# One loop in place of three for two graph layers, with the LSTM's first unit inside it

## The chip, the cores and the metric

The kernel runs on one NeuronCore of a Trainium2 chip. The metric is the device time of one execution in microseconds (us). The engines meant below are TensorE (PE in the rows; its weight loads are PEld), VectorE (DVE), ScalarE (ACT) and GpSimd (POOL). Each works through its own list of instructions in order and waits for the others at semaphores.

## The reference

`x` is 32 x 256 x 128 in fp32 (32 batches, 256 nodes, 128 features) and `adj` is 256 x 256. Two layers are added to x one after the other, each behind a layer norm and a relu. U holds the eigenvectors of the normalised Laplacian of `adj`; the second layer is two graph products and then four LSTMs over windows of nodes:

```python
h = jnp.maximum(_layernorm(x, axis=-1), 0.0)
agg = jnp.einsum('mn,bnd->bmd', U.T, h)
x = x + jnp.einsum('nm,bmd->bnd', U, jax.nn.relu(agg @ W1 + b1) @ W2 + b2)
h = jnp.maximum(_layernorm(x, axis=-1), 0.0)
h = jax.nn.relu(jnp.einsum('ts,bsh->bth', adj, h @ Wg0 + bg0))
h = jax.nn.relu(jnp.einsum('ts,bsh->bth', adj, h @ Wg1 + bg1))
for p in range(1, MAX_SKIP + 1):
    ...
    last = _lstm_last(Wih[p - 1], Whh[p - 1], bih[p - 1], bhh[p - 1], wins)
    ...
    h = h.at[:, idx, :].set(last.reshape(Bv, nw, Hd))
x = x + h
```

`wins` are the windows of p neighbouring nodes (`MAX_SKIP` is 4), and `idx` the last node of each.

## The kernel before

The eigenvectors take the kernel's first 1,128 us: tridiagonalisation, root finding, back-transformation. The change leaves that part alone. What follows are three stages, all in fp32, and all held in SBUF.

**Units of work.** The 32 batches go in 16 pairs (`PAIRS`) and 8 groups of four (`GROUPS`). Every matmul that the program asks for shows as two records in the trace. Three kinds of work stand on TensorE:

- an aggregation: for one pair, H of the pair times a 256 x 256 matrix, eight records of 256 columns (line 791, whatever the matrix: U in the first layer, adj transposed in the second);
- a weight product: for one pair, the evacuated aggregation times a 128 x 128 weight, eight records of 128 columns (line 807 in the first layer, 833 in the second's first half), or two of 512 columns (line 846 in its second half);
- an eigenvector product: for one group, UT times O, eight records of 512 columns in two halves, one PSUM bank each (line 818).

**First layer**, lines 798 to 819. In step c TensorE issues aggregation c, weight product c-1, and at odd c from 3 the eigenvector product of group (c-3)/2. ScalarE evacuates each aggregation with bias and relu (line 560). VectorE adds the bias of each weight product (line 1324, semaphore `l0_os`), adds the eigenvector product into X (1332), and takes the second layer norm's statistics of a group (1338 to 1343). ScalarE takes the root (564), and VectorE normalises the group one odd step later (`norm2`, lines 1311 to 1318); ScalarE then applies the relu (569). The eigenvector product of a group waits for `l0_os` of its two pairs, the second of which is the weight product issued just ahead of it:

```python
if c >= 3 and c % 2:
    gr = (c - 3) // 2
    pe.wait_ge(S["l0_os"], 2 * gr + 2)
```

**Second layer**, lines 821 to 846: a loop of 17 steps for each half, each with aggregation c and weight product c-1. On ScalarE, one step of the first half is the evacuation of aggregation c (line 572) and then the relu of pair c (574), which is there only when weight product c is done and VectorE has added its bias (1348):

```python
act.wait_ge(S["l1_agg"], c + 1)
a(aggs[:, c % 2], bank[c % 2][:], ACT.Copy).then_inc(S["l1_aggs"], 1)
act.wait_ge(S["l1_ys"], c + 1)
a(H[:, :, 2 * c:2 * c + 2], H[:, :, 2 * c:2 * c + 2], ACT.Relu).then_inc(S["l1_y"], 1)
```

The second half does the same with lines 577, 1352 and 580.

**LSTM**, lines 855 to 879. Units of work (one pair, one window length p, one step t) go in a fixed order, four pairs in turn. Unit u on TensorE is three gate products (four at t > 0) of 256 columns or fewer; ScalarE applies the gate functions (592) and, one unit later, the tanh of the cell (599); VectorE multiplies (1388 to 1394) and writes the hidden state (1371, 1373). The first four units wait for the relu of all 16 pairs; a later one waits for the unit four before it.

Of the kernel before, what the change touches and what calls it, by code (L numbers as in the profile page):

```python
# [33 lines left out]
def gnn_kernel(nc, x, adj, W1, b1, W2, b2, Wg0, bg0, Wg1, bg1, Wih, Whh, bih, bhh, out):  # L34
# [34 lines left out]
    with ExitStack() as ctx:  # L69
# [353 lines left out]
        def _(act):  # L423
# [131 lines left out]
            for c in range(PAIRS + 5):  # L555
# [9 lines left out]
                if c >= 6 and c % 2 == 0:  # L565
                    gr = (c - 6) // 2
# [8 lines left out]
            for c in range(PAIRS):  # L575
                act.wait_ge(S["l1_agg2"], c + 1)
                a(aggs[:, c % 2], bank[4 + c % 2][:], ACT.Copy).then_inc(S["l1_agg2s"], 1)
                act.wait_ge(S["l1_zs"], c + 1)
                v = HT[:, 2 * c:2 * c + 2]
                a(v, v, ACT.Relu).then_inc(S["l1_z"], 1)  # L580
# [22 lines left out]
        def _(pe):  # L603
# [182 lines left out]

            def aggregate(dst, c, M):
# [8 lines left out]
            for c in range(PAIRS + 2):  # L796
# [4 lines left out]
                if 1 <= c <= PAIRS:  # L801
                    e = c - 1
                    pe.wait_ge(S["l0_hids"], e + 1)
                    if e >= 2:
                        pe.wait_ge(S["l0_os"], e - 1)
                    for j in range(4):
                        last = mm(bank[4 + e % 2][:, j * P:(j + 1) * P], hid[:, e % 2, j * P:(j + 1) * P], W2s[:], start=True, stop=True)
                    last.then_inc(S["l0_o"], 1)
                if c >= 3 and c % 2:
                    gr = (c - 3) // 2  # L810
# [9 lines left out]

            for c in range(PAIRS + 1):
                if c < PAIRS:
                    pe.wait_ge(S["ln2_relu"], c + 1)
                    if c >= 2:
                        pe.wait_ge(S["l1_aggs"], c - 1)
                    aggregate(c % 2, c, adjT).then_inc(S["l1_agg"], 1)
                if c >= 1:
                    e = c - 1
                    pe.wait_ge(S["l1_aggs"], e + 1)
# [5 lines left out]
            for c in range(PAIRS + 1):  # L835
                if c < PAIRS:
                    pe.wait_ge(S["l1_y"], c + 1)
                    if c >= 2:
                        pe.wait_ge(S["l1_agg2s"], c - 1)
                    aggregate(4 + c % 2, c, adjT).then_inc(S["l1_agg2"], 1)  # L840
                if c >= 1:
                    e = c - 1
# [12 lines left out]
            pe.wait_ge(S["wlt_cp"], 8)  # L855
            for u, (gr, (p, t, part), q) in enumerate(UNITS):
                c = SLOTS * gr + q
                n = 256 if p == 1 else 2 * (N // p)
                if u < SLOTS:
                    pe.wait_ge(S["l1_z"], PAIRS)  # L860
                else:
                    pe.wait_ge(S["gate_act"], u + 1 - SLOTS)
                    if p > 1:
                        pe.wait_ge(S["h_rdy"], u + 1 - SLOTS)
                if (p, t) == (3, 0):
                    pe.wait_ge(S["third_rdy"], gr + 1)
# [555 lines left out]
```

## Time and profile before

| what | value |
|---|---|
| median of 3 runs | 1660.71 us (1658.88 to 1660.86) |
| the profiled execution's own time | 1660.92 us |
| its span in the trace, first to last instruction | 1658.9 us |
| first aggregation of the first layer (line 791) | 1128.2 us from the span's start |
| first gate function of the LSTM (line 592) | 1325.14 us |
| mean granted TensorE clock | 0.94 of full speed |

The stages that the change touches take the 197 us between the two marks of the fourth and fifth row. Times in rows are in us from the start of the span. In a timeline row the first number is the start, the second the length (to the end of the last of the xN instructions, for matmuls with the time in which the result leaves the array), and the bracket says how long the engine sat idle before it and who released it.

### The profile page before, as it was taken

The page shows a single profiled execution, that of the slowest core. Times are in us where ns is not written, and L with a number is a line of the kernel's source. Part 1 is how long each engine was busy: PE and PEld are TensorE (multiplying, and loading weights), DVE is VectorE, ACT ScalarE, POOL GpSimd, SP SyncE. Part 2 cuts the span into 40 slices and gives each one's busy share as a digit, 9 for nine tenths or more (in the row PEclk, how much of TensorE's full clock was granted, in tenths as well). Part 3 has the DMA queues.
Part 4 walks back from the last instruction along what each step waited for, and adds up shares of the span by engine and source line. Part 5 has one row for each costly group of instructions (what it writes and reads, how often), then busy time and mean ns, then how long its engine had stood idle before and what let it go on. Part 6 is the DMA issues. An engine that isn't in the chain of part 4 may idle for free.

```text
span 1658.9 us, 25312 instructions
## 1 busy us (share of the span) xinstructions
PE 1289.4 (78%) x5985; PEld 1068.8 (64%) x5985; DVE 1259.3 (76%) x6154; ACT 609.9 (37%) x2116; POOL 397.7 (24%) x2138
## 2 busy tenths in 40 slices
PE   6999999999976667777264444519878899999997
PEld 5777888888865555555143333507656588889897
DVE  7898988888888888888999999993732255555555
ACT  1222222222233444222121212402223386868676
POOL 5333333333345555555100000120000011000100
PEclk9999999999999999999887775769989999999999
DMA  7000000000000000000000000000000000000001
GB/s 166 1 1 1 1 1 1 2 1 1 2 1 1 1 1 1 1 1 1 0 1 0 1 0 1 1 0 1 1 1 1 0 1 1 1 1 26 1 27 52
DMA packets 23402, 12.64 MB, mean 8 GB/s; under 512 B 5075, under 2 KB 22230, under 8 KB 23254
## 3 DMA queue, kind: packets, MB, share of 16 engines
q1 hardware_dynamic: 23254, 11.03, 2.7%
q8 instruction: 48, 0.79, 0.2%
q14 instruction: 100, 0.82, 0.2%
HBM read 6.83 MB, written 4.19 MB: 7 GB/s over the span
## 4 chain that ended last, share of the span: by engine, by line
DVE 47%; PE 33%; issue 9%; POOL 6%; ACT 4%; DVEq 1%; POOLq 0%
PE bank L873 10%; PE bank L875 6%; DVE A L1001 4%; DVE RC L1089 4%; PE bank L647 3%; DVE O L1097 3%; PE bank L650 3%; DVE O L983 3%; DVE pa L1085 3%; DVE O L1093 2%; DVE junk L953 2%; DVE zc L995 2%; DVE wk L987 2%; PE bank L791 2%; PE bank L818 2%
## 5 line engine op out<-in xcount | busy, mean ns | idle before, releaser
L592 ACT ACTIVATE H<-bank,gate_b 128x128 f32<-128x128 f32 (+2 forms) x624 | 213.4, 438 | 81.9 <-PE bank L875 79.3
L650 PEld LDWEIGHTS bank<-O 128*128 128x128 f32 x764 | 201.3, 344 | 0.0
L873 PE MATMUL bank<-O,WlT 128*128 128x128 f32 (+1 forms) x896 | 192.0, 328 | 7.8 <-DVE O L1366 5.6
L659 PE MATMUL bank<-O,y 128*128 128x2 f32 x510 | 142.4, 349 | 65.5 <-DVE y L953 59.7
L647 PE MATMUL bank<-ident,O 128*128 128x128 f32 x382 | 148.2, 457 | 47.6 <-DVE O L983 35.6
L467 ACT ACTIVATE ncp<-pc,RC 128x2 f32<-128x2 f32 (+1 forms) x254 | 74.9, 295 | 292.4 <-DVE RC L974 292.4
L659 PEld LDWEIGHTS bank<-O,y 128*128 128x128 f32 x510 | 128.4, 312 | 77.5 <-issue 72.4
L875 PE MATMUL bank<-H,WlT 128*128 128x128 f32 (+2 forms) x768 | 169.1, 301 | 0.0
L873 PEld LDWEIGHTS bank<-O,WlT 128*128 128x128 f32 x896 | 148.1, 192 | 24.6 <-issue 7.3
L650 PE MATMUL bank<-O 128*128 128x1 f32 x764 | 162.7, 305 | 0.0
L667 PE MATMUL bank<-ident,pc 128*128 128x128 f32 x381 | 147.7, 456 | 5.4 <-DVE pc L972 2.2
L647 PEld LDWEIGHTS bank<-ident,O 128*128 128x128 f32 x382 | 60.1, 198 | 135.2 <-DVE O L983 135.2
L463 ACT ACTIVATE root<-bank 128x1 f32<-128x1 f32 x255 | 43.7, 171 | 260.1 <-PE bank L650 260.1
L735 PE MATMUL bank<-chg,fold 128*128 128x512 bf16 x64 | 28.6, 571 | 139.4 <-DVE chg L1047 139.4
L309 POOL TENSOR_TENSOR ym<-y,below 128x2 f32<-128x2 f32 (+1 forms) x254 | 49.1, 193 | 349.7 <-DVE y L961 251.8
L875 PEld LDWEIGHTS bank<-H,WlT 128*128 128x128 f32 x768 | 124.7, 189 | 3.3
L991 DVE SCALAR_TENSOR_TENSOR A<-bank,cx,A 128x254 f32<-128x254 f32 (+63 forms) x380 | 121.2, 319 | 0.4 <-issue 0.4
L418 POOL COPY Wl<-O 128x344 f32<-128x344 f32 (+1 forms) x24 | 17.2, 763 | 421.3 <-DVE O L1371 421.3
L1001 DVE SCALAR_TENSOR_TENSOR A<-bank,zc,A 128x254 f32<-128x254 f32 (+63 forms) x380 | 111.7, 321 | 4.5
L1391 DVE TENSOR_TENSOR H<-H 128x128 f32<-128x128 f32 (+2 forms) x96 | 31.6, 329 | 106.6 <-ACT H L592 106.6
L508 ACT ACTIVATE sgn<-O 128x1024 bf16<-128x1024 f32 (+1 forms) x24 | 32.2, 1342 | 205.4 <-DVE O L1097 205.4
L735 PEld LDWEIGHTS bank<-chg,fold 128*128 128x128 bf16 x64 | 5.5, 116 | 150.9 <-DVE chg L1047 121.0
(381 smaller groups left out, 3059.2 us busy)
## 6 DMA issues: line engine op xcount, KB each, us to landing
X<-in_x SPq DMA_DIRECT2D x2, 2048.0 KB, 13.9
out<-X SPq DMA_DIRECT2D x32, 128.0 KB, 1.9
adj_sb<-in_adj SPq DMA_DIRECT2D x1, 256.0 KB, 3.0
W1s<-in_L_gnn_W SPq DMA_DIRECT2D x1, 64.0 KB, 10.2
W2s<-in_L_gnn_W SPq DMA_DIRECT2D x1, 64.0 KB, 3.2
Wg0s<-in_L_gnn_Wg SPq DMA_DIRECT2D x1, 64.0 KB, 3.0
Wg1s<-in_L_gnn_Wg SPq DMA_DIRECT2D x1, 64.0 KB, 3.6
Wl<-in_L_gnn_Wih SPq DMA_DIRECT2D x1, 0.5 KB, 6.6
```

Of the source, the lines that this page charges most:

```text
L467: a(ncp[:, bs], pc[:, bs], ACT.Identity, scale=RC[:, k, 1:2]).then_inc(S["ncp_ready"], 1)
L592: ins = a(gates[:, q, i, 0:n], gate_at(p, q, i), fn, bias=gate_b[:, p - 1, i:i + 1])
L647: ins = nc.tensor.transpose(xb[:, b * P:(b + 1) * P], R[:, b, k, 0:1].to_broadcast([P, P]), idf)
L650: ins = mm(bank[0][:, 0:1], R[:, b, k, 0:1].to_broadcast([P, P]), R[:, b, k, 0:1], start=(b == bl[0]), stop=(b == 1))
L659: ins = mm(sb_[:, 0:2], y[:, 1:2].to_broadcast([P, P]), R[:, 1, k, :], start=True, stop=(k >= P - 1))
L667: ins = nc.tensor.transpose(bank[5][:, b * P:(b + 1) * P], pc[:, b:b + 1].to_broadcast([P, P]), idf)
L873: last = mm(gate_at(p, q, i), WlT[:, 0, p - 1, i, :], window(c, p, t, part), start=True, stop=(t == 0))
L875: last = mm(gate_at(p, q, i), WlT[:, 1, p - 1, i, :], hst[:, q, 0:n], start=False, stop=True)
L983: stt(out=R[:, bs, k + 1, 0], in0=cx[:, bs], scalar=gqn[:], in1=tm[:, bs], op0=ALU.mult, op1=ALU.subtract, reverse1=True).then_inc(S["x_re ...
L991: stt(out=A[:, b, c0 + 1:e], in0=bank[5][:, c0 + 1:e], scalar=cx[:, b:b + 1], in1=A[:, b, c0 + 1:e], op0=ALU.mult, op1=ALU.add).then_inc(S ...
L1001: stt(out=A[:, b, c0 + 1:e], in0=xb[:, c0 + 1:e], scalar=zc[:, b:b + 1], in1=A[:, b, c0 + 1:e], op0=ALU.mult, op1=ALU.add).then_inc(S["upd ...
L1089: mark(stt(out=pb2[:, :, 0:w], in0=lam2, scalar=dbh[:, BLK + j:BLK + j + 1], in1=pair(j, w), op0=ALU.subtract, op1=ALU.mult))
```

## The change

One loop over 3 x 16 + 1 steps takes the place of the three loops on TensorE, ScalarE and VectorE (the last two with slightly different bounds). The first layer is steps 0 to 16 and more, the second layer's halves start at steps 16 and 32. Within it:

- the eigenvector product of group g moves from odd step 2g+3, behind the weight product, to even step 2g+4, behind the aggregation and ahead of the weight product;
- on VectorE the two additions of the eigenvector product stand ahead of the bias addition (line 1324) and the statistics in the even step; ScalarE's roots move to odd steps, VectorE's `norm2` to odd steps from 5, behind the bias addition;
- in the second layer, ScalarE's relu of a pair stands two steps behind the evacuation of the same pair, not right behind it;
- the next half's aggregations start while the last weight products, and at the first seam the last eigenvector products and layer norms, are still to come;
- gate products of unit 0 are issued ahead of the last weight product; units 1 to 3 wait for the relu of their own pair and for the last reader of their banks.

No instruction that computes is added or removed. The diff, cut where the same edit is repeated:

```diff
@@ ScalarE @@
-            for c in range(PAIRS + 5):
+            for c in range(3 * PAIRS + 2):
                 if c < PAIRS:
                     ...
-                if c >= 4 and c % 2 == 0 and (c - 4) // 2 < GROUPS:
-                    gr = (c - 4) // 2
+                if PAIRS <= c < 2 * PAIRS:
+                    i = c - PAIRS
+                    act.wait_ge(S["l1_agg"], i + 1)
+                    if i >= 2:
+                        act.wait_ge(S["l1_y_ps"], i - 1)
+                    a(aggs[:, i % 2], bank[i % 2][:], ACT.Copy).then_inc(S["l1_aggs"], 1)
+                if 2 * PAIRS <= c < 3 * PAIRS:
+                    i = c - 2 * PAIRS
+                    act.wait_ge(S["l1_agg2"], i + 1)
+                    if i < 2:
+                        act.wait_ge(S["l1_y_ps"], PAIRS - 1 + i)
+                    else:
+                        act.wait_ge(S["l1_z_ps"], i - 1)
+                    a(aggs[:, i % 2], bank[4 + i % 2][:], ACT.Copy).then_inc(S["l1_agg2s"], 1)
+                gr = (c - 5) // 2
+                if c >= 5 and c % 2 and gr < GROUPS:
                     act.wait_ge(S["ln2_stats"], gr + 1)
                     ...
-            for c in range(PAIRS):
-                act.wait_ge(S["l1_agg"], c + 1)
-                a(aggs[:, c % 2], bank[c % 2][:], ACT.Copy).then_inc(S["l1_aggs"], 1)
-                act.wait_ge(S["l1_ys"], c + 1)
-                a(H[:, :, 2 * c:2 * c + 2], H[:, :, 2 * c:2 * c + 2], ACT.Relu).then_inc(S["l1_y"], 1)
...
+                if PAIRS + 2 <= c < 2 * PAIRS + 2:
+                    i = c - PAIRS - 2
+                    act.wait_ge(S["l1_ys"], i + 1)
+                    a(H[:, :, 2 * i:2 * i + 2], H[:, :, 2 * i:2 * i + 2], ACT.Relu).then_inc(S["l1_y"], 1)
+                if c >= 2 * PAIRS + 2:
+                    i = c - 2 * PAIRS - 2
+                    act.wait_ge(S["l1_zs"], i + 1)
+                    v = HT[:, 2 * i:2 * i + 2]
+                    a(v, v, ACT.Relu).then_inc(S["l1_z"], 1)
@@ TensorE @@
-            for c in range(PAIRS + 2):
+            for c in range(3 * PAIRS + 1):
                 if c < PAIRS:
                     ...
                     aggregate(c % 2, c, U).then_inc(S["l0_agg"], 1)
-                if c >= 3 and c % 2:
-                    gr = (c - 3) // 2
+                if c >= 4 and c % 2 == 0 and (c - 4) // 2 < GROUPS:
+                    gr = (c - 4) // 2
                     pe.wait_ge(S["u_cp"], 2)
                     pe.wait_ge(S["l0_os"], 2 * gr + 2)
                     ...
+                if 1 <= c <= PAIRS:
+                    e = c - 1
                     ...
+                if PAIRS <= c < 2 * PAIRS:
+                    i = c - PAIRS
+                    pe.wait_ge(S["ln2_relu"], i + 1)
+                    if i >= 2:
+                        pe.wait_ge(S["l1_aggs"], i - 1)
+                    else:
+                        pe.wait_ge(S["l0_hids"], PAIRS - 1 + i)
+                    aggregate(i % 2, i, adjT).then_inc(S["l1_agg"], 1)
+                if 2 * PAIRS <= c < 3 * PAIRS:
+                    i = c - 2 * PAIRS
+                    pe.wait_ge(S["l1_y"], i + 1)
+                    if i >= 2:
+                        pe.wait_ge(S["l1_agg2s"], i - 1)
+                    aggregate(4 + i % 2, i, adjT).then_inc(S["l1_agg2"], 1)
+                if PAIRS < c <= 2 * PAIRS:
+                    e = c - PAIRS - 1
                     pe.wait_ge(S["l1_aggs"], e + 1)
                     if e >= 2:
                         pe.wait_ge(S["l1_ys"], e - 1)
                     ...
+                if 2 * PAIRS < c:
+                    e = c - 2 * PAIRS - 1
+                    if e + 1 == PAIRS:
+                        pe.wait_ge(S["wlt_cp"], 8)
+                        gate_products(0)
                     pe.wait_ge(S["l1_agg2s"], e + 1)
                     ...
             for u, (gr, (p, t, part), q) in enumerate(UNITS):
-                if u < SLOTS:
-                    pe.wait_ge(S["l1_z"], PAIRS)
+                if u:
+                    if u < SLOTS:
+                        pe.wait_ge(S["l1_z"], q + 1)
+                        pe.wait_ge(*(None, (S["l1_ys"], PAIRS), (S["l1_agg2s"], PAIRS), (S["l1_zs"], PAIRS))[u])
                     ...
+                    gate_products(u)
@@ VectorE @@
-            for c in range(1, PAIRS + 2):
+            for c in range(1, 3 * PAIRS + 1):
+                gr = (c - 4) // 2
+                if c >= 4 and c % 2 == 0 and gr < GROUPS:
                     ...
                 if c <= PAIRS:
                     ...
-                    if gr:
-                        norm2(gr - 1)
                     ...
-            norm2(GROUPS - 1)
+                gr = (c - 5) // 2
+                if c >= 5 and c % 2 and gr < GROUPS:
+                    dve.wait_ge(S["ln2_root"], gr + 1)
                     ...
+                if PAIRS < c <= 2 * PAIRS:
+                    e = c - PAIRS - 1
+                    dve.wait_ge(S["l1_y_ps"], e + 1)
                     ...
+                if c > 2 * PAIRS:
+                    e = c - 2 * PAIRS - 1
+                    dve.wait_ge(S["l1_z_ps"], e + 1)
                     ...
```

## Rows read from the trace of the kernel before

**Rows 1.** The page of the profiled execution, part 1: busy time, share of the span, instructions.

```profile
PE 1289.4 (78%) x5985; PEld 1068.8 (64%) x5985; DVE 1259.3 (76%) x6154; ACT 609.9 (37%) x2116; POOL 397.7 (24%) x2138
```

**Rows 2.** Stretches of the trace: their length, busy time of each engine, granted TensorE clock.

```profile
1138.00:1190.00 52.00, 48.36 (x213) 34.12 (x212) 35.67 (x144) 11.62 (x23) 0.00 (x0) 1.00 0.00 1
...
1199.00:1211.00 12.00, 6.74 (x17) 3.28 (x16) 6.59 (x29) 1.25 (x3) 0.00 (x0) 0.72 0.00 1
...
1211.00:1229.30 18.30, 12.24 (x50) 10.10 (x48) 9.04 (x38) 5.22 (x10) 0.00 (x0) 0.81 0.00 1
...
1269.40:1319.60 50.20, 45.40 (x166) 29.67 (x166) 11.06 (x16) 17.95 (x32) 0.00 (x0) 1.00 0.00 0
...
1319.60:1325.20 5.60, 4.05 (x9) 2.72 (x10) 0.69 (x1) 1.97 (x3) 0.00 (x0) 0.75 0.01 3
```

**Rows 3.** Timeline of the eigenvector layer, TensorE: start, length, work, idle time before it.

```profile
1141.43 1.89 PE L791 MATMUL bank<-A,H 128*128 128x256 f32 x8
...
1143.16 1.05 PE L807 MATMUL bank<-W2s,Wl 128*128 128x128 f32 x8
...
1146.67 3.60 PE L818 MATMUL bank<-O,V 128*128 128x512 f32 x8
...
1150.11 1.89 PE L791 MATMUL bank<-A,H 128*128 128x256 f32 x8
...
1156.41 3.67 PE L818 MATMUL bank<-O,V 128*128 128x512 f32 x8 [0.91 <-issue]
...
1189.38 1.89 PE L791 MATMUL bank<-A,H 128*128 128x256 f32 x8
```

**Rows 4.** Timeline of the same layer, VectorE, within one group of four batches.

```profile
1160.12 0.69 DVE L1332 TENSOR_TENSOR X<-X,bank 128x512 f32<-128x512 f32 x1 [1.03 <-PE bank L818]
...
1160.96 2.14 DVE L1316 TENSOR_SCALAR H<-X,mv,stats 128x128 f32<-128x128 f32 x8
...
1165.45 1.28 DVE L1324 TENSOR_TENSOR O<-bank,xjunk 128x512 f32<-128x512 f32 x2
```

**Rows 5.** Timeline of the seam from the eigenvector layer to the graph layer, TensorE.

```profile
1199.19 1.05 PE L807 MATMUL bank<-W2s,Wl 128*128 128x128 f32 x8
...
1205.50 5.76 PE L818 MATMUL bank<-O,V 128*128 128x512 f32 x8 [5.26 <-issue]
...
1220.57 2.08 PE L833 MATMUL bank<-Wg0s,Wl 128*128 128x128 f32 x8 [5.86 <-ACT Wl L572]
...
1229.29 1.16 PE L833 MATMUL bank<-Wg0s,Wl 128*128 128x128 f32 x8 [0.20 <-ACT Wl L572]
```

**Rows 6.** Timeline of the graph layer: the last round, and its very last product.

```profile
1266.34 1.16 PE L833 MATMUL bank<-Wg0s,Wl 128*128 128x128 f32 x8 [0.20 <-ACT Wl L572]
...
1267.54 0.69 DVE L1348 TENSOR_TENSOR H<-bank,bg0m 128x512 f32<-128x512 f32 x1 [2.40 <-PE bank L833]
...
1268.80 0.58 ACT L572 ACTIVATE Wl<-bank 128x512 f32<-128x512 f32 x1
...
1269.43 1.16 PE L833 MATMUL bank<-Wg0s,Wl 128*128 128x128 f32 x8 [1.93 <-ACT Wl L572]
...
1319.61 1.13 PE L846 MATMUL bank<-Wl,Wg1s 128*128 128x512 f32 x2 [1.93 <-ACT Wl L577]
```

**Rows 7.** Timeline of the seam to the LSTM and of its first units.

```profile
1321.50 0.63 ACT L580 ACTIVATE O<-O 128x512 f32<-128x512 f32 x1 [1.94 <-DVE O L1352]
...
1322.15 1.28 ACT L592 ACT_TABLE_LOAD   x1
...
1325.14 1.21 ACT L592 ACTIVATE H<-bank,gate_b 128x256 f32<-128x256 f32 x3 [1.71 <-PE bank L873]
...
1326.83 1.21 ACT L592 ACTIVATE H<-bank,gate_b 128x256 f32<-128x256 f32 x3 [0.48 <-PE bank L873]
...
1336.48 1.35 ACT L592 ACTIVATE H<-bank,gate_b 128x256 f32<-128x256 f32 x3
...
1340.14 0.30 PEld L873 LDWEIGHTS bank<-O,WlT 128*128 128x128 f32 x2 [0.24 <-issue]
```

More of the change, by code:

```diff
@@ L785, in _, with gate_products @@
             mm256(3, Zk, QTp).then_inc(S["u_ps"], 1)
+            def gate_products(u):
+                gr, (p, t, part), q = UNITS[u]
+                c = SLOTS * gr + q
+                n = 256 if p == 1 else 2 * (N // p)
+                for gt in ("f", "i", "g", "o"):
+                    if gt == "f" and t == 0:
+                        continue
+                    i = GATE[gt]
+                    last = mm(gate_at(p, q, i), WlT[:, 0, p - 1, i, :], window(c, p, t, part), start=True, stop=(t == 0))
+                    if t:
+                        last = mm(gate_at(p, q, i), WlT[:, 1, p - 1, i, :], hst[:, q, 0:n], start=False, stop=True)
+                last.then_inc(S["gate_ps"], 1)
             def aggregate(dst, c, M):
@@ L800, in _ @@
                     aggregate(c % 2, c, U).then_inc(S["l0_agg"], 1)
[L801 to L808, printed above, removed]
-                if c >= 3 and c % 2:
-                    gr = (c - 3) // 2
+                if c >= 4 and c % 2 == 0 and (c - 4) // 2 < GROUPS:
+                    gr = (c - 4) // 2
                     pe.wait_ge(S["u_cp"], 2)
@@ L819, in _ @@
                         last.then_inc(S["l0_x"], 1)
[L821 to L827, printed above, removed]
-                    e = c - 1
+                if 1 <= c <= PAIRS:
+                    e = c - 1
+                    pe.wait_ge(S["l0_hids"], e + 1)
+                    if e >= 2:
+                        pe.wait_ge(S["l0_os"], e - 1)
+                    for j in range(4):
+                        last = mm(bank[4 + e % 2][:, j * P:(j + 1) * P], hid[:, e % 2, j * P:(j + 1) * P], W2s[:], start=True, stop=True)
+                    last.then_inc(S["l0_o"], 1)
+                if PAIRS <= c < 2 * PAIRS:
[14 more added lines that the diff above has]
+                    e = c - PAIRS - 1
                     pe.wait_ge(S["l1_aggs"], e + 1)
@@ L1309, in _ @@
             dve.wait_ge(S["biases"], 3)
-            def norm2(gr):
-                dve.wait_ge(S["ln2_root"], gr + 1)
-                link(v.reciprocal(stats2[:, :, 4 * gr:4 * gr + 4, 0], rstd2[:, :, 4 * gr:4 * gr + 4]))
-                for i in range(4 * gr, 4 * gr + 4):
+            for c in range(1, 3 * PAIRS + 1):
+                gr = (c - 4) // 2
+                if c >= 4 and c % 2 == 0 and gr < GROUPS:
                     for b in range(NB):
-                        ins = ts(H[:, b, i], X[:, b, i], mv2[:, b, i, 0:1], stats2[:, b, i, 0:1], ALU.subtract, ALU.mult)
-                    if i % 2:
-                        ins.then_inc(S["ln2_norm"], 1)
-            for c in range(1, PAIRS + 2):
+                        i = NB * gr + b
+                        dve.wait_ge(S["l0_x"], i + 1)
+                        xs = X[:, b, 4 * gr:4 * gr + 4, :]
+                        tt(xs, xs, bank[6 + i % 2][:].rearrange("p (a d) -> p a d", a=4), ALU.add).then_inc(S["l0_y"], 1)
                 if c <= PAIRS:
@@ L1325, in _ @@
                        b2bc[:].unsqueeze(1).unsqueeze(1).to_broadcast([P, NB, 2, D]), ALU.add).then_inc(S["l0_os"], 1)
-                if c >= 3 and c % 2:
-                    gr = (c - 3) // 2
-                    for b in range(NB):
-                        i = NB * gr + b
-                        dve.wait_ge(S["l0_x"], i + 1)
-                        xs = X[:, b, 4 * gr:4 * gr + 4, :]
-                        tt(xs, xs, bank[6 + i % 2][:].rearrange("p (a d) -> p a d", a=4), ALU.add).then_inc(S["l0_y"], 1)
-                    if gr:
-                        norm2(gr - 1)
+                if c >= 4 and c % 2 == 0 and gr < GROUPS:
                     dve.wait_ge(S["l0_y"], NB * (gr + 1))
```

62 lines of the change are left out of this document (20 added, 42 removed).

## The prediction

> **What bounds the kernel now.** I read the page's busy times first, then stretches of the stages that the change touches, then the timeline of each, following who releases whom. Over the whole span TensorE and VectorE are about equally busy [rows 1], but that mixes stages. In the stretches from 1138 to 1320 us TensorE is the busiest, at 90% or more where the work runs steadily (48.36 of 52.00, 45.40 of 50.20), and only 56% at the first seam (6.74 of 12.00); VectorE is at 69% and 22%, ScalarE at 22% and 36% [rows 2]. So TensorE is the limit here, and what it loses is waits, plus a granted clock of 0.72 and 0.75 of full speed (a mixture of its levels of 2.4 and 1.2 GHz) at the two seams, after it stood idle [rows 2].
>
> **Prices of TensorE's work.** Start to start, an aggregation is 1143.16 - 1141.43 = 1.73 us and an eigenvector product 1150.11 - 1146.67 = 3.44. The group that begins at 1141.43 runs with no wait and takes 8.68; it holds two aggregations, two weight products and one eigenvector product, so a weight product is (8.68 - 3.44) / 2 - 1.73 = 0.89 [rows 3]. The second half's weight product is two records of 512 columns, a quarter of the eigenvector product: 0.86. A unit of the LSTM's p = 1 is six records of 256 columns, 6/8 of an aggregation: 1.30.
>
> **Part 1, eigenvector product one aggregation later.** The first group has no `norm2` in it; in the later ones the eigenvector product waits 0.91 [rows 3]. It waits for `l0_os` of the pair just multiplied, and VectorE, in its order, comes to that addition only after normalisation and statistics, 5.3 us behind its addition into X (1160.12 to 1165.45) [rows 4]. Before, the six rounds from 1141.43 to the weight product at 1199.19 take 57.76 [rows 3, 5]; their work is 6 x 8.68 = 52.08. After, the product needs only pairs whose addition is one step older. I work one period out, from the start of the even step. TensorE: aggregation to 1.73, first half of the eigenvector product to 3.45, second to 5.17, weight product to 6.06, aggregation to 7.79, weight product to 8.68. VectorE: additions into X at 3.7 and 5.4; bias addition at 6.3 (it needs the weight product, 0.2 after its end); statistics to about 9.4; bias addition to 10.0; normalisation to 12.3. Its next addition into X is due at 8.68 + 3.7 = 12.4. As a check, VectorE's same work in rows runs from 1160.12 to 1165.45 + 1.28 = 6.61, with one more addition of 0.69: 7.3 in a period of 8.68 [rows 4]. It idles about 1.1 us between the two halves and catches up there. The additions that TensorE needs are 3 us or more early. ScalarE has 11.62 of 52.00 [rows 2]. TensorE bound, gain 57.76 - 52.08 = **5.7**. If VectorE were 1.1 us a group slower than I think, this cover is gone and the period grows towards the old one; the bound is a gain of 0.
>
> **Part 2, first seam.** Before, from the weight product at 1199.19 to the third one of the second layer at 1229.29 is 30.10 [rows 5], with waits of 5.26 (VectorE's statistics stand ahead of the bias addition) and 5.86 (the last group's layer norm), the rest half-clock work. The work in it is three weight products, one eigenvector product and four aggregations: 2.67 + 3.44 + 6.92 = 13.03. After, aggregations of the second layer, whose layer norms are long done, stand where TensorE waited; the layer norm of group 7 is needed only by its 15th aggregation. What could hold it is queued elsewhere: ScalarE's evacuation stands behind a relu that waits for a `norm2`, and its root for group 6 behind an evacuation. From the start of step 16 by the same prices: VectorE ends the normalisation of group 5 at 3.7, statistics of group 6 at 8.3; ScalarE evacuates at 8.0, takes the root at 8.6; VectorE normalises group 6 to 11.3, adds the first bias to 12.0, then the eigenvector product, group 7's statistics and the second bias to 16.4; root at 17.2, normalisation of group 7 to 19.8, third bias to 20.5. TensorE needs the first bias at 16.5, the second at 19.1, the third at 21.7. It waits for none; the least margin is 1.2 us. Gain 30.10 - 13.03 = **17.1**. The lower bound, with the layer norm's wait of 5.86 come back and the clock lost behind it, is some 5.
>
> **Part 3, second layer.** Its round of 3.09 (1266.34 to 1269.43) is a loop through three engines: weight product, bias addition 1.20 later, relu, evacuation at 2.46 to 3.04, next weight product [rows 6]. ScalarE's relu of pair c stands ahead of the evacuation of pair c+1, though TensorE finished that long before. With the relu two steps later the loop is open: the evacuation starts when the aggregation ends (0.2 behind it) and TensorE has another 1.73 of aggregation before it needs it. ScalarE then has 0.58 + 0.63 and VectorE 0.69 in a round of 2.62. Before, from 1229.29 to the last weight product at 1319.61: 90.32 [rows 5, 6]. Work: 14 weight products of 0.89, 28 aggregations, 15 products of 0.86: 12.46 + 48.44 + 12.90 = 73.80. The two waits of 1.93 at the halves' ends [rows 6] are in the difference. Gain **16.5**. A half-hidden loop would leave some of it; I see no other loop, and take all.
>
> **Part 4, into the LSTM.** The path before: last weight product 1319.61, relu 1321.50 (1.89), activation table load 1322.15 to 1323.43, then ScalarE idles 1.71 for gate products that could start only behind the last relu and ran with the clock at 0.75 in that stretch [rows 2, 7]; first gates 1325.14, second unit's 1326.83. From there ScalarE is the limit: seven units in 9.65 us, 1.38 each, with no idle, against 1.30 of TensorE, and it sets TensorE's first long unit at 1340.14 [rows 7], which waits for the hidden state of unit 8. Behind that the order is untouched, and I carry the shift to the end one for one. After: gate products of unit 0 cost 1.30 ahead of the last weight product; then 1.89 + 0.65 + 1.28 to the end of the load, first gates at once, second after 1.21 (the row's length): 6.33 against 1326.83 - 1319.61 = 7.22. Gain **0.9**. TensorE's other 11 units take 14.3 from the end of the last weight product, ScalarE's chain reaches the long unit some 3 later, so the limit stays ScalarE.
> No row shows a gate function right behind a table load; the nearest starts 1.71 behind one, so the hidden remainder of a load is between 0 and 1.71. I take 0, because 1325.14 is also where the products of unit 0 end. The Trainium skill, "ScalarE: Activation LUTs", What ACT_TABLE_LOAD costs, gives 1.28 us for the load, which the row confirms, and another 1.38 of drain, which no row here can confirm or refute. By that page the first gates would come 1.38 later, and the total would be 1622.0.
>
> **Sum.** 5.7 + 17.1 + 16.5 + 0.9 = 40.2 us. The profiled execution took 1660.92, so 1660.9 - 40.2 = 1620.7; its time is 0.2 above the median of the runs, so the median after is forecast at **1620.5**, 2.4% faster. Other added waits (for evacuations at the halves' starts, for the weights' transposes, for each pair's relu in units 1 to 3) are for things finished several us earlier, except unit 3's for the last bias addition, there 0.9 behind the last weight product, when TensorE has 2.6 of units 1 and 2 to do.
>
> **Rivals.**
> - *Table load with a remainder* (above): up to 1.71, so 1620.5 to 1622.2. For it: it would be invisible before. Chance 0.14.
> - *VectorE becomes the bound of the first layer.* Its chain of 8.6 to 8.7 is as long as the period once its wait in the middle is counted. Against: that wait of 1.1 absorbs. Price up to 5.7: 1621.6 to 1626.2. Chance 0.07.
> - *The seam does not close*: ScalarE's or VectorE's queue holds TensorE in steps 18 to 22, as the margins are 1.2 us, and if the idle is long the clock falls as it did at 1199 [rows 2]. Price 1 to 12: 1621.5 to 1632. That is also how the change would not do what it says. Chance 0.08.
> - *Slower than before: the clock.* If the new order left short waits in each step and the clock stayed at 1.2 GHz, the 143 us of work from 1138 to the LSTM would take as long again: 1620.5 + 143 = 1764. It decides from 40 us of full-speed work at half clock. Against: waits of 0.9 per 9.8 us and 0.5 per 3.1 us leave the clock at 1.00 [rows 2, 3, 6], and the new order has fewer. The Trainium skill, "TensorE: Matmul & The Clock Gate", A second HAM failure mode, says that frequent micro-idles between groups that cycle through PSUM banks make the clock swing; this trace, cycling through banks with such idles, does not agree. Chance 0.02.
> - The forecast: 0.69. Its own range is 1618.5 to 1622.5.
>
> **Range and chances.** The range takes in the table load, most of the two middle rivals, and a few us below, since a chip may run the whole kernel 0.1 to 0.2% quicker (the three runs before span 2 us): 1617 to 1626. About 0.2% is what a measurement of this kernel can tell. Faster 0.96, within 0.2% 0.01, slower 0.03 (the clock, and what I have not thought of).
>
> **What the profile after would show.** A period of 8.68 between the starts of even steps from 1138.0, with no idle ahead of line 818's successor; step 16 at 1190.1; no TensorE idle over 0.3 us from there to the last weight product at about 1281.5; rounds of 2.62 and 2.59; clock 1.00 throughout; relu of the last pair at 1283.4, gates at 1285.3 (1286.7 if a load has a remainder), the first long unit near 1300. VectorE's additions into X starting right behind normalisation, with no gap before the first and about 1 us before the second. The prediction is wrong if TensorE waits for VectorE in a steady step, if it idles in steps 17 to 22, or if the LSTM takes longer from its first gates than the 333.8 us before.

## The result, and the profile after

The changed kernel takes **1620.51 us** (median of 4 runs, 1619.17 to 1620.93) against 1660.78 of the kernel before (4 runs, 1658.88 to 1661.1). The ratio is 0.9758 with a 95% interval of 0.9742 to 0.9775: 40 us or 2.4% faster. The forecast was 1620.5. That its last digit fits is luck: two terms behind it were each off by about 1 us, in opposite directions, as shown below.

In the kernel after, line 816 is the aggregation, 835 the eigenvector product, 843, 865 and 875 the three weight products (807, 833, 846 before), 807 and 809 the gate products (873 and 875 before). First the page's busy times, which answer to [rows 1].

```profile
PE 1270.4 (78%) x5985; PEld 1064.2 (66%) x5985; DVE 1260.1 (78%) x6154; ACT 610.8 (38%) x2116; POOL 397.6 (25%) x2138
```

The busy shares hardly moved. The stretches of the timeline, which answer to [rows 2] (columns as there), say more: from 1138 us to the LSTM, TensorE has work in every microsecond, at a granted clock of 1.00.

```profile
1138.00:1190.00 52.00, 52.00 (x240) 37.67 (x239) 41.02 (x171) 15.66 (x28) 0.00 (x0) 1.00 0.00 1
1190.00:1213.00 23.00, 23.00 (x118) 18.26 (x117) 18.34 (x72) 9.02 (x19) 0.00 (x0) 1.00 0.00 1
1213.00:1282.00 69.00, 69.00 (x332) 55.93 (x331) 18.34 (x27) 29.64 (x53) 0.00 (x0) 1.00 0.00 1
...
1286.00:1301.00 15.00, 12.88 (x53) 10.64 (x52) 7.53 (x20) 14.12 (x41) 0.00 (x0) 0.89 0.00 1
```

The first layer in the steady state, against [rows 3, 4]:

```profile
1137.06 1.89 PE L816 MATMUL bank<-A,H 128*128 128x256 f32 x8
...
1155.86 2.14 DVE L1362 TENSOR_SCALAR H<-X,mv,stats 128x128 f32<-128x128 f32 x8
...
1156.14 3.60 PE L835 MATMUL bank<-O,V 128*128 128x512 f32 x8
...
1158.06 0.69 DVE L1340 TENSOR_TENSOR X<-X,bank 128x512 f32<-128x512 f32 x1
...
1159.77 0.69 DVE L1340 TENSOR_TENSOR X<-X,bank 128x512 f32<-128x512 f32 x1 [1.03 <-PE bank L835]
...
1164.81 3.60 PE L835 MATMUL bank<-O,V 128*128 128x512 f32 x8
```

The eigenvector products start 8.67 us apart (8.68 was forecast; in the kernel before they were 9.82 apart) and none has idle time before it. VectorE runs from the normalisation straight into its addition into X, and idles 1.03 only ahead of the second one, because the second half of TensorE's product is not done. That is the slack of about 1.1 that the prediction counted on. The first seam, against [rows 5]:

```profile
1189.10 3.60 PE L835 MATMUL bank<-O,V 128*128 128x512 f32 x8
...
1197.58 0.20 ACT L578 ACTIVATE rstd<-mv 128x8 f32<-128x8 f32 x1
...
1197.78 3.60 PE L835 MATMUL bank<-O,V 128*128 128x512 f32 x8
...
1205.56 1.05 PE L865 MATMUL bank<-Wg0s,Wl 128*128 128x128 f32 x8
...
1208.77 1.29 DVE L1368 TENSOR_TENSOR H<-bank,bg0m 128x512 f32<-128x512 f32 x2
...
1210.80 1.05 PE L865 MATMUL bank<-Wg0s,Wl 128*128 128x128 f32 x8
```

From the start of the eigenvector product in step 16 to the third weight product of the second layer are 1205.56 - 1189.10 = 16.46 us; its work by the old prices is 3.44 + 13.03 = 16.47 (the 3.44 is the eigenvector product that the change moved into this stretch). ScalarE's root for group 6 comes at 1197.58, 8.5 behind the start of the step (8.6 forecast). The bias addition of pair 2 ends at 1208.77 + 0.6 = 1209.4, 1.4 ahead of the weight product at 1210.80 that needs it (1.2 forecast). The second layer, against [rows 6]:

```profile
1229.14 1.05 PE L865 MATMUL bank<-Wg0s,Wl 128*128 128x128 f32 x8
1229.34 0.60 ACT L566 ACTIVATE Wl<-bank 128x512 f32<-128x512 f32 x1 [1.50 <-PE bank L816]
1229.83 0.62 ACT L587 ACTIVATE H<-H 128x512 f32<-128x512 f32 x1
...
1230.03 1.89 PE L816 MATMUL bank<-adjT,H 128*128 128x256 f32 x8
...
1231.76 1.05 PE L865 MATMUL bank<-Wg0s,Wl 128*128 128x128 f32 x8
```

The round is 1231.76 - 1229.14 = 2.62. The evacuation (line 566) starts when the aggregation ends, the relu behind it (587) belongs to a pair two steps older, and TensorE never waits. The seam to the LSTM, against [rows 7]:

```profile
1276.70 1.89 PE L816 MATMUL bank<-adjT,H 128*128 128x256 f32 x8
...
1280.58 1.02 PE L875 MATMUL bank<-Wl,Wg1s 128*128 128x512 f32 x2
...
1282.37 0.63 ACT L592 ACTIVATE O<-O 128x512 f32<-128x512 f32 x1 [1.52 <-DVE O L1373]
1283.01 1.28 ACT L604 ACT_TABLE_LOAD   x1
1284.31 2.30 ACT L604 ACTIVATE H<-bank,gate_b 128x256 f32<-128x256 f32 x6
...
1293.14 7.54 PE L807 MATMUL bank<-O,WlT 128*128 128x256 f32 x26 [2.12 <-DVE O L1392]
...
1295.61 1.20 ACT L604 ACTIVATE H<-bank,gate_b 128x256 f32<-128x256 f32 x3 [0.30 <-PE bank L807]
...
1297.69 1.20 ACT L604 ACTIVATE H<-bank,gate_b 128x256 f32<-128x256 f32 x3 [0.58 <-PE bank L807]
...
1300.51 0.59 PE L809 MATMUL bank<-H,WlT 128*128 128x256 f32 x2
```

Here the trace leaves the forecast. The table load of 1.28 is followed by the first gate functions after 0.02 us. But TensorE, now ahead of ScalarE, idles 2.12 us ahead of unit 8, its clock falls to a mean of 0.59 in the 2.9 us behind that and 0.89 over the stretch of 1286 to 1301, and ScalarE waits 0.30 and 0.58 for it. In the kernel before, ScalarE never waited between its second unit and the first long one.

All runs can be laid side by side by three marks of the trace: the first aggregation, the last aggregation, and TensorE's first product with a hidden state (the first long unit, at 1300.51 above). Times in us, from the starts of the matmul rows. In the kernel before these rows start at 1128.41 (the 1128.2 of the table ahead of the prediction is the start of the weight load), at 1314.46 and at 1340.68 (the prediction's 1340.14 is a weight load ahead of it):

```profile
1340.68 0.59 PE L875 MATMUL bank<-H,WlT 128*128 128x256 f32 x2
```

| kernel | first to last aggregation | last aggregation to first long unit | to the span's end | TensorE's wait ahead of unit 8, clock behind it |
|---|---|---|---|---|
| before | 186.05 | 26.22 | 318.22 | no idle row |
| after | 149.22 | 23.81 | 318.09 | 2.12, falls |
| product later (e1) | 174.31 | 27.06 | 318.29 | no idle row |
| relu lag (e2) | 171.15 | 21.96 | 318.12 | no idle row |
| both, no seams (e3) | 158.65 | 21.96 | 318.10 | no idle row |
| relu at once (e4) | 159.57 | 23.93 | 318.16 | 2.12, stays |
| relu lag one (e5) | 149.25 | 23.83 | 318.09 | 2.13, falls |
| gates after (e6) | 149.23 | 21.34 | 318.11 | 1.18, stays |
| early table (e7) | 149.22 | 21.11 | 318.11 | 1.05, stays |
| filler (e8) | 149.23 | 22.56 | 318.07 | 0.20, stays |
| table and gates (e9) | 149.23 | 20.18 | 318.11 | no idle row |
| e9 again | 149.23 | 20.18 | 318.10 | no idle row |
| three more on VectorE (e11) | 153.76 | 22.55 | 318.11 | 2.12, stays |
| changed again (e12) | 149.22 | 23.82 | 318.12 | 2.12, falls |

Ahead of the first mark all kernels run the same code, and take 1126.6 to 1129.2 us. That spread of 2.5 us is in every median, so differences of 1 to 3 us below are read from the table and not from medians. The stretches between the marks repeat to 0.03 us where a kernel was run twice.

### The profile page after: what moved, and what is told of

Its sections match the earlier page's. It is cut to its first block, busy times and chain, and to the rows that moved or that the text cites. A ratio compares the mean times of both kernels' runs of the same rounds, so it can differ in the third digit from the quotient of the medians.

```text
span 1618.6 us, 25346 instructions
## 1 busy us (share of the span) xinstructions
PE 1270.4 (78%) x5985; PEld 1064.2 (66%) x5985; DVE 1260.1 (78%) x6154; ACT 610.8 (38%) x2116; POOL 397.6 (25%) x2138
## 4 chain that ended last, share of the span: by engine, by line
DVE 47%; PE 35%; issue 8%; POOL 6%; ACT 3%; DVEq 1%; POOLq 0%
PE bank L807 10%; PE bank L809 6%; PE bank L816 5%; DVE A L1023 4%; DVE RC L1111 4%; PE bank L659 3%; DVE O L1119 3%; PE bank L662 3%; DVE O L1005 3%; DVE pa L1107 3%; DVE O L1115 2%; DVE junk L975 2%; DVE zc L1017 2%; DVE wk L1009 2%; ACT H L604 2%
```

## The experiments

**e1, the product later, alone.** The kernel before with part 1 only:

```diff
-                if c >= 3 and c % 2:
-                    gr = (c - 3) // 2
+                if c >= 4 and c % 2 == 0 and (c - 4) // 2 < GROUPS:
+                    gr = (c - 4) // 2
                     ...
+                if 1 <= c <= PAIRS:
```

(on VectorE and ScalarE as in the change). Expected:

> The kernel before with part 1 alone: the eigenvector product at even steps from 4, ahead of the weight product, with roots and normalisation at odd steps; second layer and LSTM as before. My theory: the steady period falls from 9.82 to 8.68 (5.7 us), and at the first seam the wait of 5.26 shrinks to about 1.5 because the last bias addition no longer stands behind statistics, while the wait for the last group's layer norm stays at about 6. Together 11 to 12 us: 1649 us. Rival (the moved product only moves the wait elsewhere, and the gain comes from the overlap of the layers): under 2 us, 1659 to 1661.

Measured 1649.69 us (1660.70 before on that chip), ratio 0.9936 (0.9919 to 0.9952): 11.0 us. That is the total of the first theory, and it fits by luck, as the clock shows below. TensorE's rows, start and length, with the last two eigenvector products, the second layer's first weight product, and the last weight product of each of its halves:

```profile
1189.37 3.60 PE L810 MATMUL bank<-O,V 128*128 128x512 f32 x8
...
1194.86 3.67 PE L810 MATMUL bank<-O,V 128*128 128x512 f32 x8 [1.00 <-DVE O L1322]
...
1207.46 2.08 PE L833 MATMUL bank<-Wg0s,Wl 128*128 128x128 f32 x8 [5.48 <-ACT Wl L572]
...
1255.33 1.50 PE L833 MATMUL bank<-Wg0s,Wl 128*128 128x128 f32 x8 [1.93 <-ACT Wl L572]
...
1307.20 2.08 PE L846 MATMUL bank<-Wl,Wg1s 128*128 128x512 f32 x2 [1.93 <-ACT Wl L577]
```

The wait of 5.26 is now 1.00, and the one for the last layer norm is still there with 5.48. The wait of 1.93 at the end of the second layer's first half did not cost clock in the kernel before; here it does:

```profile
1256.00:1262.00 6.00, 6.00 (x23) 4.96 (x22) 0.69 (x1) 1.23 (x2) 0.00 (x0) 0.72 0.00 0
```

Six us at a mean clock of 0.72 are 1.7 us lost against the same rows of before. Without that e1 would have gained 13.4 up to the last aggregation instead of 11.7. The wait of 1.93 at the end of the second half costs clock too: the weight product behind it takes 2.08, where it took 1.13 before, and the front of the LSTM is 0.8 longer.

**e2, the relu later, alone.** The kernel before with part 3 only, in its two separate loops of 18 steps:

```diff
-            for c in range(PAIRS):
                 ...
-                act.wait_ge(S["l1_ys"], c + 1)
-                a(H[:, :, 2 * c:2 * c + 2], H[:, :, 2 * c:2 * c + 2], ACT.Relu).then_inc(S["l1_y"], 1)
                 ...
+            for c in range(PAIRS + 2):
                 ...
+                if c >= 2:
+                    i = c - 2
+                    act.wait_ge(S["l1_ys"], i + 1)
+                    a(H[:, :, 2 * i:2 * i + 2], H[:, :, 2 * i:2 * i + 2], ACT.Relu).then_inc(S["l1_y"], 1)
```

> The kernel before with part 3 alone: in the second layer's two separate loops ScalarE's relu of a pair stands two steps behind its evacuation. My theory: rounds of 2.62 and 2.59 in place of 3.09 and 3.06, and both waits of 1.93 at the halves' ends gone, 16.5 us: 1644.3 us. Rival (the loops must be merged for it, since the ends of each half stay serial): only the rounds gain, 12 us: 1648.6.

Measured 1640.34 us, ratio 0.9881 (0.9867 to 0.9896): 20.4 us, 4 more than the first theory and far from the rival. From the third weight product to the last one it takes 1301.0 - 1227.2 = 73.8 us, the forecast work to 0.1. The rest is not the edit: 1.1 us ahead of the first mark, 1.0 by a later fall of the clock at the first seam, and 1.7 because in front of the LSTM the clock did not fall, though TensorE waits 1.54 there as it did before (1.53).

**e3, parts 1 and 3 without the seams** (the edits of e1 and e2 together).

> Parts 1 and 3 together in the kernel before, the layers still in loops of their own and the LSTM behind the last relu. My theory: the two add up, 11.5 + 16.5 = 28, so 1632.8 us, and the remaining 12 us of the change are the overlap at the first seam. Rival (they share a bottleneck or the clock): the sum is missed by more than 2 us.

Measured 1628.07 us, ratio 0.9806 (0.9791 to 0.9820): 32.6 us. The expected 28 is missed by 4.6, more than the 2 us at which the rival was to hold. But the parts do add up: e1 and e2 as measured give 11.0 + 20.4 = 31.4, and what was too small was the price of e2, by the items listed there. Up to the last aggregation e3 gains 27.4, where e1 and e2 gain 11.7 and 14.9, together 26.6: they add up to within 0.8, less than what the clock took from e1. So of the change's 36.8 us in that stretch, 9.4 belong to the overlap at the first seam (12 was expected). TensorE's rows at the end of the second layer:

```profile
1287.74 1.89 PE L801 MATMUL bank<-adjT,H 128*128 128x256 f32 x8
...
1292.98 16.89 PE L883 MATMUL bank<-O,WlT 128*128 128x256 f32 x74 [1.54 <-ACT O L590]
1309.70 0.59 PE L885 MATMUL bank<-H,WlT 128*128 128x256 f32 x2
```

All gate products stand behind the last relu, with 1.54 of waiting ahead of the first, and run at full clock (74 records in 16.89 us, 18.57 before). **This front of the LSTM takes 21.96 us from the last aggregation, the changed one 23.81.** Even where the changed one keeps its clock (e8 and e11 below) it takes 22.56 and 22.55.

**e4, the relu at once again**, in the changed kernel:

```diff
-                if PAIRS + 2 <= c < 2 * PAIRS + 2:
-                    i = c - PAIRS - 2
-                    ...
+                for i in range(PAIRS):
+                    if c == (PAIRS + 2 + i if i < 6 else max(PAIRS + i, PAIRS + 7)):
+                        ...
-                if c >= 2 * PAIRS + 2:
-                    i = c - 2 * PAIRS - 2
+                if 2 * PAIRS <= c < 3 * PAIRS:
+                    i = c - 2 * PAIRS
```

> The changed kernel, with ScalarE's relu right behind the evacuation of the same pair again, from pair 7 of the first half on and for all of the second half (earlier pairs keep the lag of two steps). My theory: the loop through three engines is back, 9 + 16 rounds of 3.09 and 3.06 in place of 2.62 and 2.59, 12 us: 1632.5. Rival (the overlap of the layers and not the lag opened the loop): 1620.5.

Measured 1631.24 us, ratio 0.9824 (0.9809 to 0.9838); 1632.5 was expected, and 1620.5 by the rival. The stretch between aggregations is 10.4 longer than in the changed kernel, and the old loop is back, 1289.20 - 1286.14 = 3.06 a round with 0.21 of idle. TensorE's rows of the timeline:

```profile
1286.14 1.12 PE L875 MATMUL bank<-Wl,Wg1s 128*128 128x512 f32 x2 [0.20 <-ACT Wl L574]
...
1289.20 1.12 PE L875 MATMUL bank<-Wl,Wg1s 128*128 128x512 f32 x2 [0.21 <-ACT Wl L574]
...
1304.94 6.27 PE L807 MATMUL bank<-O,WlT 128*128 128x256 f32 x26 [2.12 <-DVE O L1392]
```

The lag opened the loop, not the overlap. The third row matters below: the same wait of 2.12, and 26 records in 6.27 us, at full clock.

**e5, one step of lag instead of two**, in both halves (the first is shown).

```diff
-                if PAIRS + 2 <= c < 2 * PAIRS + 2:
-                    i = c - PAIRS - 2
+                if PAIRS + 1 <= c < 2 * PAIRS + 1:
+                    i = c - PAIRS - 1
                     ...
```

> The changed kernel with the relu one step behind the evacuation in both halves, not two. My theory: one step is enough to open the loop, since the bias addition of a pair ends 1.8 us after its aggregation and the next evacuation is due 2.6 after: rounds stay 2.62 and 2.59, 1620.5. Rival (the relu then waits in front of an evacuation, and TensorE for that): 0.1 to 0.5 us a round, 1622 to 1634.

Measured 1619.99 us, ratio 0.9757 (0.9744 to 0.9770), 149.25 between aggregations. One step is enough; the second buys nothing.

**e6, gate products of unit 0 behind the last weight product.**

```diff
-                    if e + 1 == PAIRS:
-                        pe.wait_ge(S["wlt_cp"], 8)
-                        gate_products(0)
                     pe.wait_ge(S["l1_agg2s"], e + 1)
                     ...
+                    if e + 1 == PAIRS:
+                        pe.wait_ge(S["wlt_cp"], 8)
+                        gate_products(0)
```

> The changed kernel with the gate products of unit 0 behind the last weight product, not ahead of it. My theory: ScalarE is the limit at the start of the LSTM, so its first gates come 1.3 us earlier after the last aggregation; TensorE then waits 1.3 less ahead of unit 8 (0.8 in place of 2.1), its clock does not fall there, and the first long unit starts about 2.3 us earlier: 1618.2. If only the order counts and the clock falls anyway: 1619.2. Rival (the change was right to put them ahead, TensorE's work being the limit): 1620.5 or later.

Measured 1618.74 us, ratio 0.9754 (0.9739 to 0.9768); behind the last aggregation 21.34, which is 2.47 less than the changed kernel (2.3 expected). TensorE's wait shrinks by 0.9 and the 26 records behind it take 6.26, not 7.54, in this row of the timeline:

```profile
1292.59 6.26 PE L807 MATMUL bank<-O,WlT 128*128 128x256 f32 x26 [1.18 <-DVE O L1392]
```

Putting unit 0 ahead delays ScalarE's last relu and its first gate functions by 1.2 us against the last aggregation, and ScalarE is the limit from there. The other 1.3 of the 2.47 are the clock.

**e7, the table load inside the second layer.**

```diff
+                if c == PAIRS + 8:
+                    a(root[:], root[:], ACT.Sigmoid)
```

> The changed kernel with one sigmoid of a 128 x 1 column on ScalarE at step 24, whose result is not used, so that the activation table of the LSTM is loaded inside the second layer. My theory: the load of 1.28 leaves the path, first gates 1.3 us earlier against the last aggregation, TensorE's wait ahead of unit 8 shrinks to 0.8 and its clock stays, 2.3 us in all: 1618.2; without the clock's part 1619.2. Rival (copy and relu are not in the sigmoid's table): the load comes back at once and again ahead of the gates, 1620.5 or more.

Measured 1618.86 us, ratio 0.9754 (0.9739 to 0.9768); 2.70 less behind the last aggregation, 1.4 of it up to the first gate functions. The load does not come back: copy and relu run with the sigmoid's table in place. The timeline from the last weight product on (lines stand two lower here):

```profile
1282.26 1.02 PE L877 MATMUL bank<-Wl,Wg1s 128*128 128x512 f32 x2
...
1284.58 2.28 ACT L606 ACTIVATE H<-bank,gate_b 128x256 f32<-128x256 f32 x6
...
1293.39 6.26 PE L809 MATMUL bank<-O,WlT 128*128 128x256 f32 x26 [1.05 <-DVE O L1394]
```

**e8, a filler in TensorE's idle time.** Four products whose results nothing reads, between the two waits of unit 8:

```diff
                         pe.wait_ge(S["gate_act"], u + 1 - SLOTS)
+                        if u == 2 * SLOTS:
+                            for _ in range(4):
+                                mm(bank[0][:, 256:512], idf, adjT[:, 0, :], start=True, stop=True)
```

> The changed kernel with four products of 256 columns, results not used, issued by TensorE between its two waits ahead of unit 8, where it sat idle 2.1 us. It adds 1.7 us of work in the idle time. My theory (the clock falls because of that idle time): granted clock 1.00 from there, ScalarE's two waits of 0.3 and 0.6 for TensorE vanish, the first long unit starts 0.9 earlier: 1619.6. Rival (the clock falls for another reason, or ScalarE's waits come from elsewhere): clock and waits as in the changed kernel, 1620.5.

Measured 1618.88 us, ratio 0.9753 (0.9737 to 0.9769); 1.25 less behind the last aggregation, from more work. The timeline, filler first:

```profile
1292.23 1.99 PE L894 MATMUL bank<-adjT,ident 128*128 128x256 f32 x8
...
1294.43 6.36 PE L807 MATMUL bank<-O,WlT 128*128 128x256 f32 x26 [0.20 <-DVE O L1395]
```

ScalarE's two waits are gone and the records behind run at full clock. From ScalarE's first gate function to the first long unit the changed kernel takes 16.20 us and e8 14.96; the 1.25 is therefore what the fall of the clock costs (0.9 was expected). The idle time is needed for the fall: e6, e7, e8 and e9, where it is shorter or gone, all keep the clock. It is not enough by itself, since e4 and e11 have the same 2.12 and keep the clock too. What else decides is not settled, and e8 has one trace, so it alone could not tell the filler from chance.

**e9, table load and gate products both moved** (the diffs of e7 and e6 together).

> Both: table load inside the second layer, and unit 0's gate products behind the last weight product. My theory: first gates 2.6 us earlier than in the changed kernel against the last aggregation; then TensorE, with 11 units of 1.30 behind the last weight product, becomes the limit nearly together with ScalarE (its wait ahead of unit 8 would be 2.1 - 2.6, below nothing), so that 3.0 to 3.3 us are gained in all: 1617.3. Rival (ScalarE alone is the limit): 2.6 + 0.9 = 3.5, 1617.0, with an idle TensorE ahead of unit 8.

Measured 1617.07 us, ratio 0.9742 (0.9727 to 0.9756); 20.18 behind the last aggregation, 3.63 less than the changed kernel. Neither expectation holds as it stood. ScalarE's first gate functions come 2.58 earlier against the last aggregation, and the clock gives back 1.25: 3.83 if ScalarE alone were the limit. The missing 0.2 is TensorE: from the first gate functions to the first long unit e9 takes 15.15, e6 14.93 and e7 14.91, and TensorE has no idle row ahead of unit 8, where the rival wanted one. So ScalarE is the limit with TensorE nearly level, as the first theory had it, but the lost clock is worth more than the 0.9 counted. The timeline from the last aggregation to the first long unit:

```profile
1277.01 1.89 PE L818 MATMUL bank<-adjT,H 128*128 128x256 f32 x8
...
1280.55 16.80 PE L809 MATMUL bank<-O,WlT 128*128 128x256 f32 x74
...
1282.04 2.50 ACT L606 ACTIVATE H<-bank,gate_b 128x256 f32<-128x256 f32 x6
...
1297.19 0.59 PE L811 MATMUL bank<-H,WlT 128*128 128x256 f32 x2
```

**e12 and e9 again**, side by side on one chip, five rounds:

> The changed kernel once more, as the partner on this chip for the run with the table load and the gate products moved: 1620.5, and in the trace 149.2 us from the first aggregation to the start of the last, 23.8 from there to the first long unit, 318.1 to the end.

> The kernel with both edits at the seam to the LSTM again, five rounds beside the changed kernel. By the traces of the first run it is 3.6 us faster behind the last aggregation: 1616.9 where the changed kernel takes 1620.5. If the first result was the spread of runs (1 us in the first 1,128 us), the difference shrinks below 1.5.

The changed kernel 1619.99 us, ratio 0.9760 (0.9746 to 0.9773); e9 1617.79, ratio 0.9742 (0.9728 to 0.9755). By medians that is 2.2 us, with intervals that just overlap; by the marks it is 3.64, as in the first run. In the two profiled executions the code ahead of the first mark took 2 us more in e9, which is more than the difference between the two readings. e9 is the best version found. In e12 the clock fell at the same place as in the first run.

**e11, three more operations a group on VectorE**, 128 x 512 each, results not used:

```diff
                     ts(mv2[:, :, 4 * gr:4 * gr + 4, 1], mv2[:, :, 4 * gr:4 * gr + 4, 1], EPS, None, ALU.add).then_inc(S["ln2_stats"], 1)
+                    for d in (junk2, Vh, Rm)[:3]:
+                        tt(d[:], ident[:], below[:], ALU.mult)
```

> The changed kernel with three more additions-like operations of 128 x 512 on VectorE behind the statistics of each group, results not used, some 0.6 to 0.7 us each, so 1.8 to 2.1 a group. My theory: VectorE's slack in a period is only its idle time, 1.03 + 0.20 us, so the period of 8.67 grows by 0.6 to 0.9 in six or seven groups and the first seam loses 1 to 2 us more: 1625 to 1629. Rival (VectorE is busy 79% of this stretch, so 1.8 us in 8.67 fit in): 1620.5.

Measured 1624.31 us, ratio 0.9781 (0.9768 to 0.9795). That is just below the expected 1625 to 1629 and clear of the rival's 1620.5, but the mechanism was not the expected one. In the first layer TensorE's period stays 8.67 (timeline, two eigenvector products and one of the added operations):

```profile
1174.19 3.60 PE L835 MATMUL bank<-O,V 128*128 128x512 f32 x8
...
1175.02 0.69 DVE L1357 TENSOR_TENSOR Rm<-ident,below 128x512 f32<-128x512 f32 x1
...
1182.86 3.60 PE L835 MATMUL bank<-O,V 128*128 128x512 f32 x8
```

VectorE now needs 8.92 us a group (additions into X at 1169.59 and 1178.51), and falls behind by 0.25 each time: of the 1.80 added, 1.55 found room, more than the 1.23 of idle time expected. TensorE does not feel it, since it reads those bias additions 3 us later. The bill comes at the seam, in one piece, as the timeline shows:

```profile
1210.83 0.68 DVE L1370 TENSOR_TENSOR H<-bank,bg0m 128x512 f32<-128x512 f32 x1
...
1211.65 1.13 PE L865 MATMUL bank<-Wg0s,Wl 128*128 128x128 f32 x8 [2.61 <-DVE H L1370]
...
1212.62 3.50 PE L816 MATMUL bank<-adjT,H 128*128 128x256 f32 x8
```

The weight product waits 2.61 for a bias addition, and the aggregation behind it takes 3.50 at half clock; 153.76 - 149.22 = 4.5 us in all, of which 1.3 come back because the clock then stays up in front of the LSTM. So in the steady state VectorE can overrun the period, and TensorE feels nothing before the seam. The wait falls on the fourth weight product of the second layer. In the changed kernel that one has 2.9 us to spare (its bias addition runs at 1204.57 to 1205.25, the product starts at 1208.18); e11 delays the addition by 5.6, counted from the first mark, by what VectorE is behind and by the three operations that stand ahead of it. The fifth has the smallest margin, 1.4, but e11 does not test it by itself.

## Why the prediction was right, point by point

- **Part 1, right.** Forecast 5.7: from the fifth aggregation to the start of the eigenvector product of step 16 the change takes 1189.10 - 1137.06 = 52.04 against 52.08. e1 shows that this part needs nothing of the others.
- **Part 2, right.** Forecast 17.1, measured 30.10 - (16.46 - 3.44) = 17.1. The least margin of 1.2 us, worked out, measures 1.4; e11 shows that a VectorE late enough does hold TensorE at this seam. By e1 and e3 the 17.1 splits: some 7.7 come with the product moved (its wait of 5.26 becomes 1.00, and behind the shorter wait it runs at full clock, 3.67 us for 5.76), the remaining 9.4 need the layers overlapped.
- **Part 3, right.** Forecast 16.5: from the third weight product to the last are 75.02 us, of which 1.30 are unit 0, so 73.72 against 73.80 forecast and 90.32 before. e2 shows it alone, e4 takes it back.
- **Part 4, mis-sized, and its sign wrong.** Forecast a gain of 0.9. From the last weight product to the first long unit were 21.07 us and are 19.93; with unit 0's 1.30 ahead of it that is a loss of 0.2. The step that failed is "ScalarE's chain reaches the long unit some 3 later, so the limit stays ScalarE": those 3 us, in which TensorE has nothing to do, were put at no cost. ScalarE's chain came out as worked, even a little shorter: with the clock kept, in e8, it is 18.68 from the last weight product, and with unit 0's 1.30 that is a gain of 1.1. But TensorE idles for 2.12, and the fall of the clock behind that costs 1.25. The prediction had a fall of the clock only as a rival for the layers, never for the place where TensorE gets ahead. One of its own signs of being wrong did show: from the first gate functions to the end the LSTM takes 334.3 us, longer than the 333.8 before.
- **The missing term, luck.** The common part ahead of the first mark took 0.9 less in this profiled execution, within its spread of 2.5. Between the first mark and the first long unit the change gains 39.2; with 1.1 from outside these marks that is the 40.3 by which the span shrank. The 1.1 has nothing to do with the change and happens to make up for what part 4 lost.
- **The shift carried to the end one for one, right**: 318.22 before, 318.07 to 318.29 in all runs.

The rivals: a remainder behind the table load is ruled out (0.02 us to the first gate function, against up to 1.71). The 1.38 us of drain of the Trainium skill, "ScalarE: Activation LUTs", What ACT_TABLE_LOAD costs, are not there in this trace, neither ahead of the load nor behind it; the measurement decides. VectorE did not become the bound; by e11 even 1.80 us more a group does not make it one within the first layer. The seam closed with no wait. The clock stayed at 1.00 through both layers.

That the change pays is thus three findings: an operation waiting for something that the releasing engine's queue puts last (part 1), a loop through three engines closed by one operation's place in a queue (part 3), and 9.4 us of overlap at one seam. The edit at the other seam, taken by itself, is worth less than nothing: e3's plain front is 1.85 us quicker than the changed one (0.6 where the changed one keeps its clock), e9's 3.6.

## What to carry to other kernels

Where an engine of a pipeline waits at a steady beat, look for the operation in the releasing engine's queue that stands ahead of one long ready, and move it one step; e5 shows that one step can be enough. Price a schedule by hand from start-to-start times, with each engine's order written out for one period and for each seam: that gave three terms here to 0.1 us. At a seam where the limit passes from one engine to another, put the new limit's work first, and count what the old one does with its idle time: here a wait of 2 us on TensorE cost another 1.25 in clock.

## What the runs showed of the hardware that was not expected

- TensorE's granted clock can fall from 2.4 to 1.2 GHz after a wait of about 2 us between steady work, and need not. Of five traces with a wait of 2.12 or 2.13 ahead of unit 8 the clock fell in three (after, e5, e12) and stayed at 1.00 in two (e4, e11). The wait of 1.93 at the end of the second layer's first half cost clock in e1 and not in the kernel before. In the kernel before the clock fell behind a wait of 1.93 and one of 1.53 with a single weight product between them; in e2 and e3, with a wait of 1.54 alone, it stayed. With waits of 1.18 or less ahead of unit 8 it never fell.
- The activation table load takes 1.28 us, and the next function follows 0.02 us later. In e7 and e9 it was moved into the second layer, and copy and relu ran on the sigmoid's table.
